# Keys and values projected on 64-row tiles, side by side on the two halves of TensorE's rows

## The chip, the cores and the metric

The kernel runs on one core of one Trainium2 chip. The metric is the device time of the program in microseconds (us), as the median of several runs. A profiled execution has a span (from the first to the last instruction) and its own time, which is a little longer than its span.

## The reference

A gated cross-attention block and a mixture of experts, in float32. There are 32 batches of 56 query tokens and 1500 context tokens, 256 channels, 16 heads of 16.

```
x = x + tanh(g_xattn) * layernorm(rs * (softmax(q k^T / 4, masked) v  @ Wo.T + bo)) * gamma + beta
      with q = layernorm(x) @ Wq.T + bq,  k = ctx @ Wk.T + bk,  v = ctx @ Wv.T + bv
x = x + tanh(g_ffn) * sum over 2 of 8 experts of w_e * (relu(layernorm(x) @ w_fc[e])**2 @ w_proj[e])
```

Scores are scaled by 1/4 and clipped to -50..50, and the two experts of a token come from a softmax over its two largest router logits.

## The kernel before

**Tiling.** The batches are worked on in 16 pairs (`NP`). A batch's 1500 context tokens are three groups of 500 (`TG`), a group is four chunks of 125 (`TC`). So a pair has 6 groups (`PG`) and 24 chunks (`PC`), and its loop runs over `UN` = 12 steps u = 0 to 11. A step works on two chunks, and on half of the projections of the group that comes next. Context arrives already transposed (channels on the partitions), in 500 KB transfers into `raw`.

**Precision.** Float32 products are made of three fp32r products: each operand is split into a rounded part (hi) and a remainder (lo), and hi x hi, hi x lo and lo x hi are summed in PSUM. This goes for keys, values, scores and experts.

**A step on TensorE** (`pair`): scores of two chunks (`scores`: 24 matmuls, each with 64 rows of keys as weights and 224 columns of masked queries moving; the two halves of the rows write two different banks), then `k_proj` (six matmuls: 128 rows, 128 output rows, 500 columns), then `v_proj` (twelve matmuls: 128 rows, 125 tokens as weights, 256 columns moving), then in some steps one of five side operations, then `pv` of the two chunks of the step before (probabilities times values; 17 output rows each, four in a quadrant each, with a column of ones that gives the softmax sums). Side operations use PSUM tile `side_ps`, which is bank 0 of `k_ps`: `spread_sums` at u=1, `x_transpose` at u=3, `q_proj` at u=5, `out_proj` at u=7, `y_transpose` at u=11. In the first pair and in the last some of them are missing, so each runs 15 times.

**ScalarE**: the exponential of each chunk (`exps`), the rounded keys (`k_hi_evac`), the rounded context (`ctx_high`, once in two steps), and evacuations of side operations. **VectorE**: the clip of the probabilities (`clip`), the remainders of context and keys (`ctx_low`, `k_lo_evac`), values plus bias from PSUM (`v_evac_step`, into `vst`), and in `before_clips` the small work of layer norm, query splitting and normalisation, by step. **GpSimd**: three inverse square roots in a pair, the remainder of the expert weights, x plus beta. Every engine works its queue in the order in which the code is written; semaphores tie them together. TensorE's program is unrolled, those of ScalarE, VectorE and SyncE loop over pairs.

**Waits that matter here.** `v_proj` may start when `v_evac` says that VectorE has emptied the one bank of `v_ps`; `k_proj` when `k_lo` says so of its bank; the next use of bank 0 after a side operation waits for that one's evacuation (the table `freed`). `spread_sums` waits for `sum_split`, which VectorE gives after `o_evac_step` and `sums_split` of the last PV. `delta` on VectorE waits for `out_proj`.

After the attention loop, seven groups of 256 tokens go through 8 experts each; the change doesn't touch that phase.

Of the kernel before, what the change touches and what calls it, by code (L numbers as in the profile page):

```python
# [16 lines left out]
P = 128  # L17
KD = D // P
# [35 lines left out]
def gated_cross_attention_moe(nc, a, x1_dram, out):  # L54
# [5 lines left out]
    with ExitStack() as ctx:  # L60
# [136 lines left out]
        ctx_split = sem("ctx_split")  # L197
        kproj_done = sem("kproj_done")
        vproj_done = sem("vproj_done")
        k_hi = sem("k_hi")  # L200
        k_lo = sem("k_lo")
        v_evac = sem("v_evac")
# [163 lines left out]
        def _(pe):  # L366
# [19 lines left out]
            def v_proj(n, half, s):  # L386
# [8 lines left out]
                                   wv_hi[:, k, :], wv_lo[:, k, :], k == 0, k == KD - 1)  # L395
                last.then_inc(vproj_done, 1)

            def scores(i, c):

                n = i * PC + c  # L400
                b, g = c // NC, c // GC
                if c % NC == 0:
                    pe.wait_ge(q_ready, 4 * i + 2 * b + 2)
                if c % GC == 0:
                    pe.wait_ge(k_lo, KD * (i * PG + g + 1))
                wait(pe, exp_done, n - 1)
                cs = slice(c % GC * TC, (c % GC + 1) * TC)
                for m in range(KD):
                    for term, (k, q) in enumerate(((kh, q_hi), (kh, q_lo), (kl, q_hi))):
                        for r in range(2):  # L410
# [64 lines left out]
            def pair(i, first=False, final=False):  # L475
                freed = {}
                if not first:
                    freed.update({0: (ylo_done, i), 2: (sum_evac, i), 8: (dlt_evac, i)})
                if not final:
                    freed.update({4: (xT_done, i + 2), 6: (qT_done, i + 2)})  # L480
                for u in range(UN):
                    q, half = divmod(u, 2)
                    n = i * PG + q + 1
                    more = not (final and q == PG - 1)
                    scores(i, 2 * u)
                    if first and u == 0:
                        pe.wait_ge(v_evac, 2)
                    scores(i, 2 * u + 1)
                    if more:
                        k_proj(n, half, (q + 1) % 2, freed.get(u))  # L490
                        v_proj(n, half, (q + 1) % 2)
                        if half == 1:
                            pe.wait_ge(k_lo, KD * n + 1)
                    if u == 1 and not first:
                        spread_sums(i - 1)
                    if u == 3 and not final:
                        x_transpose(i + 1)
                    if u == 5 and not final:
                        q_proj(i + 1)
                    if u == 7 and not first:  # L500
                        out_proj(i - 1)
                    if u == 10 and final:
                        pe.wait_ge(ylo_done, NP - 1)
                        pe.wait_ge(wr_split, 18)
                        pe.wait_ge(k_lo, KD * B * NG)
                        for t in range(RT):
                            router(0, t)
                    if u == 11 and not first:
                        y_transpose(i - 1)
                    if first and u == 1:  # L510
                        pe.wait_ge(o_clear, 1)
                    if not (first and u == 0):
                        for d in (2, 1):
                            pv(*((i, 2 * u - d) if u > 0 else (i - 1, PC - d)))
# [76 lines left out]
        def _(act):  # L591
# [7 lines left out]
            def ctx_high(n, s, count):  # L599

                act.wait_ge(raw_in[s], 16 * count)
                wait(act, vproj_done, 2 * (n - 1))
                act.activation(c_hi[:, s, :, :], raw[:, s, :, :], ACT.Copy).then_inc(ctx_hi, 1)

# [52 lines left out]
            def pair(i, first=False, final=False):  # L657
                for u in range(UN):
                    q, half = divmod(u, 2)
                    if u == 0 and not final:  # L660
                        load_xq(i + 1)
                    if u == 10:
                        if not first:
                            store_x1(i - 1)
                        load_xr(i)
                        if not final:
                            load_matrix(i + 1)
                    if half == 0 and not (final and q >= PG - 2):
                        ctx_high(i * PG + q + 2, q % 2, i * NG + q // 2 + 2)
                    exps(i, 2 * u)  # L670
                    exps(i, 2 * u + 1)
                    if not (final and q == PG - 1):
                        k_hi_evac(i * PG + q + 1, half, (q + 1) % 2)
                    if u == 1:
                        if not first:
                            sums_spread(i - 1)
                        expert_hi(i)
                    if u == 3 and not final:
                        x_transposed(i + 1)
                    if u == 11 and not first:  # L680
                        y_transposed(i - 1)
                    if u == 11 and final:
                        second_of_two(0)

# [52 lines left out]
        def _(dve):  # L737
# [179 lines left out]
            def pair(i, first=False, final=False):  # L917
                for u in range(UN):
                    q, half = divmod(u, 2)
                    before_clips(i, u, first, final)  # L920
                    if not (final and q >= PG - 2):
                        ctx_low(i * PG + q + 2, half, q % 2)
                    clip(i, 2 * u)
                    clip(i, 2 * u + 1)
                    if not (final and q == PG - 1):
                        k_lo_evac(i * PG + q + 1, half, (q + 1) % 2)
                        v_evac_step(i * PG + q + 1, half, (q + 1) % 2)
                if not first:
                    y_low(i - 1)

            def before_clips(i, u, first, final):

# [21 lines left out]
                    inverse(i - 1, 3)  # L954
                if u == 5 and not first:
                    divide(i - 1)
                if u == 6 and not final:
                    q_evac(i + 1)
                    q_split(i + 1, 0)
                if u == 7:  # L960
                    o_evac_step(i, 0)
                    sums_split(i, 0)
                    if not final:
                        q_high(i + 1, 0)
                if u == 8:
                    if not first:
                        delta(i - 1)
# [168 lines left out]
```

## Time and profile before

| | |
|---|---|
| time, 3 runs | median 1268.37 us (1267.36 to 1270.18) |
| profiled execution | 1267.26 us, span 1265.1 us |
| TensorE matmuls (PE) | 1248.7 us busy, 99% of the span |
| TensorE weight loads (PEld) | 1129.9 us, 89% |
| VectorE (DVE) | 964.8 us, 76% |
| ScalarE (ACT) | 688.5 us, 54% |
| GpSimd (POOL) | 174.6 us, 14% |
| HBM read and written | 60.77 MB and 3.67 MB, 51 GB/s over the span |
| mean granted TensorE clock | 0.997 of full speed |

The attention loop takes some 1070 us of the span, the experts the last 180. Busy time of PE is modelled, since matmuls overlap: the starts of matmuls and weight loads tell more than their durations. A weight load (LDWEIGHTS) brings the stationary operand into the array, and the matmul behind it streams the moving one.

### The profile page before, as it was taken

What the parts mean: (1) busy time and instruction counts of PE and PEld (TensorE: products, weight loads), DVE (VectorE), ACT (ScalarE), POOL (GpSimd) and SP (SyncE); (2) the same over time, 40 slices, a digit from 0 to 9 for tenths busy, and PEclk for the clock granted to TensorE, in tenths of its full rate; (3) what the DMA queues carried; (4) which work ended last, traced back from release to release, by engine and by line L of the source; (5) the groups of instructions that cost most, each with busy time, mean ns of one, the idle gap of its engine ahead of it and who ended that gap; (6) DMA issues with size and microseconds to landing.
All of it is one profiled execution on the core that took longest, in us unless ns stands there. A gap on an engine that the chain in (4) does not pass through costs nothing.

```text
span 1265.1 us, 51469 instructions
## 1 busy us (share of the span) xinstructions
PE 1248.7 (99%) x22040; PEld 1129.9 (89%) x22040; DVE 964.8 (76%) x1806; ACT 688.5 (54%) x854; POOL 174.6 (14%) x142
## 2 busy tenths in 40 slices
PE   7999999999999999999999999999999999899998
PEld 6888888888888888888888888888888888899998
DVE  6678777878787877787777878787878777687555
ACT  5555555556555556565555555565555565344443
POOL 1000101010101010010001010101010100154443
PEclk9999999999999999999999999999999999899999
DMA  5121212121112112121211121211121120010000
GB/s 158 52 67 43 64 53 70 53 66 56 55 51 68 55 42 71 47 70 53 70 50 57 53 70 53 67 55 54 51 69 55 45 74 5 19 64 10 17 8 17
DMA packets 29507, 68.19 MB, mean 54 GB/s; under 512 B 6037, under 2 KB 13458, under 8 KB 29330
## 3 DMA queue, kind: packets, MB, share of 16 engines
q1 hardware_dynamic: 20450, 54.61, 14.2%
q10 hardware_dynamic: 8880, 10.75, 2.6%
q8 instruction: 168, 2.75, 0.9%
q14 instruction: 9, 0.07, 0.0%
HBM read 60.77 MB, written 3.67 MB: 51 GB/s over the span
## 4 chain that ended last, share of the span: by engine, by line
PE 94%; issue 2%; DVE 1%; POOL 1%; ACT 0%; DMA 0%; DVEq 0%; POOLq 0%; ACTq 0%
PE sc_ps L412 23%; PE o_ps L427 14%; PE k_ps L369 10%; PE v_ps L370 7%; PE v_ps L369 7%; PE v_ps L371 7%; PE k_ps L371 7%; PE k_ps L370 7%; PE sc_ps L369 3%; PE sc_ps L370 3%; PE sc_ps L371 3%; PE k_ps L444 1%; POOL h_lo L352 1%; PE k_ps L457 1%; DVE h_sq L1043 0%
## 5 line engine op out<-in xcount | busy, mean ns | idle before, releaser
L610 ACT ACTIVATE prob<-sc_ps,m_bias 125x896 f32<-125x896 f32 x384 | 366.3, 1005 | 321.8 <-PE sc_ps L412 321.8
L915 DVE TENSOR_SCALAR prob<-prob 125x896 f32<-125x896 f32 x384 | 245.1, 642 | 140.8 <-ACT prob L610 137.4
L412 PE MATMUL sc_ps<-q_hi,kh 64*125 64x224 f32 x1536 | 228.5, 294 | 0.0
L370 PE MATMUL v_ps<-wv_lo,c_hi 128*125 128x256 f32 x764 | 214.8, 281 | 0.0
L369 PE MATMUL v_ps<-wv_hi,c_hi 128*125 128x256 f32 x764 | 214.3, 280 | 0.0
L371 PE MATMUL v_ps<-wv_hi,c_lo 128*125 128x256 f32 x764 | 214.0, 280 | 0.0
L412 PE MATMUL sc_ps<-q_hi,kl 64*125 64x224 f32 x1536 | 209.8, 270 | 0.0
L412 PE MATMUL sc_ps<-q_lo,kh 64*125 64x224 f32 x1536 | 209.3, 269 | 0.0
L427 PE MATMUL o_ps<-prob,vst 125*17 125x56 f32 x12288 | 189.2, 214 | 0.0
L427 PEld LDWEIGHTS o_ps<-prob,vst 125*17 125x17 f32 x12288 | 158.3, 98 | 31.5 <-issue 9.8
L763 DVE SCALAR_TENSOR_TENSOR kl<-k_ps,cst,kh 128x500 fp32r<-128x500 f32 x192 | 141.5, 738 | 46.5 <-ACT kh L597 44.7
L369 PE MATMUL k_ps<-c_hi,wk_hi 128*128 128x500 f32 x384 | 169.7, 442 | 0.9 <-DVE c_lo L769 0.9
L412 PEld LDWEIGHTS sc_ps<-q_hi,kh 64*125 64x125 f32 x1536 | 144.8, 185 | 17.7 <-issue 0.2
L597 ACT ACTIVATE kh<-k_ps,cst 128x500 fp32r<-128x500 f32 x192 | 130.5, 680 | 43.3 <-PE k_ps L371 41.0
L371 PE MATMUL k_ps<-c_hi,wk_lo 128*128 128x500 f32 x384 | 149.6, 390 | 0.0
L370 PE MATMUL k_ps<-c_lo,wk_hi 128*128 128x500 f32 x384 | 149.3, 389 | 0.0
L370 PEld LDWEIGHTS v_ps<-wv_lo,c_hi 128*125 128x125 f32 x764 | 141.8, 186 | 7.6
L369 PEld LDWEIGHTS v_ps<-wv_hi,c_hi 128*125 128x125 f32 x764 | 141.9, 186 | 7.2
L316 POOL TENSOR_TENSOR rstd<-var_e,mhalf 112x1 f32<-112x1 f32 x48 | 69.2, 1442 | 560.1 <-DVE var_e L753 560.1
L412 PEld LDWEIGHTS sc_ps<-q_hi,kl 64*125 64x125 f32 x1536 | 145.9, 187 | 0.0
L412 PEld LDWEIGHTS sc_ps<-q_lo,kh 64*125 64x125 f32 x1536 | 145.4, 186 | 0.0
L371 PEld LDWEIGHTS v_ps<-wv_hi,c_lo 128*125 128x125 f32 x764 | 141.9, 186 | 0.0
(129 smaller groups left out, 1913.7 us busy)
## 6 DMA issues: line engine op xcount, KB each, us to landing
raw<-in_ctxT SPq DMA_DIRECT2D x96, 500.0 KB, 3.5
w_raw<-in_we ACTq DMA_DIRECT2D x16, 256.0 KB, 3.7
xq<-in_x ACTq DMA_DIRECT2D x16, 112.0 KB, 2.0
xr<-in_x ACTq DMA_DIRECT2D x16, 112.0 KB, 3.6
x_scratch<-x ACTq DMA_DIRECT2D x16, 112.0 KB, 3.7
out_y<-acc SPq DMA_DIRECT2D x7, 256.0 KB, 2.0
acc<-x_scratch SPq DMA_DIRECT2D x1, 1280.0 KB, 6.3
rec<-rec SPq DMA_DIRECT2D x64, 14.0 KB, 2.3
```

What stands on the lines that cost most here:

```text
L316: pool.tensor_tensor(rstd[ln][0:PW, :], var_e[ln][0:PW, :], mhalf[0:PW, :], ALU.pow)\
L352: pool.tensor_tensor(h_lo[:, e % NB, :, :], h_sq[:, e % 2, :, :], plain(h_hi[:, e % NB, :, :]), ALU.subtract).then_inc(hlo_done, 1)
L369: pe.matmul(ps, w_h, m_h, start=first, stop=False)
L370: pe.matmul(ps, w_h, m_l, start=False, stop=False)
L371: return pe.matmul(ps, w_l, m_h, start=False, stop=last)
L412: last = pe.matmul(sc_ps[0:TC, 2 * (c % 2) + r, m * HS * S:(m + 1) * HS * S], k[rows, g % 2, m, cs], q[rows, b, m, :, :], start=term == 0, ...
L427: last = pe.matmul(o_ps[q * 32:q * 32 + VW, col * S:(col + 1) * S], vst[0:TC, c // GC % 2, c % GC, h, :], prob[0:TC, c % PB, at * S:(at + ...
L444: last = pe.matmul(bank[:, m * PW:(m + 1) * PW], wq[:, k, m * P:(m + 1) * P], xnT[:, k, :], start=(k == 0), stop=(k == KD - 1))
L597: act.activation(kh[:, s, m, :], k_ps[:, m, 0:TG], ACT.Identity, bias=bk[:, m:m + 1]).then_inc(k_hi, 1)
L610: act.activation(prob[0:TC, c % PB, :].rearrange("p (c n) -> p c n", c=2), sc_ps[0:TC, 2 * (c % 2):2 * (c % 2) + 2, 0:NH * S // 2], ACT.Ex ...
L763: dve.scalar_tensor_tensor(kl[:, s, m, :], k_ps[:, m, 0:TG], bk[:, m:m + 1], plain(kh[:, s, m, :]), ALU.add, ALU.subtract).then_inc(k_lo, 1)
L915: dve.tensor_scalar(p, p, EXP_LO, EXP_HI, ALU.max, ALU.min).then_inc(clip_done, 1)
```

## The change

Keys and values of a half group are computed by `kv_part`, in two parts. In part 0 the key matmuls use rows 0 to 63 (the first 64 of each 128 input channels) and the value matmuls rows 64 to 127; in part 1 it is the other way round, and each bank ends with the whole sum. Within a part the order is value (first chunk), key, value (second chunk), six times over. Part 0 stands at the head of a step, ahead of the first chunk's scores, part 1 between the two chunks' scores. The side operations now follow part 0. New semaphores `kpart_done` and `vpart_done` keep part 1 from starting before part 0 is complete, as both write the same banks. ScalarE and VectorE are reordered to suit: evacuations of keys and values stand between the two exponentials (clips), values ahead of the keys' remainder; evacuations of side operations, `q_evac` and `delta` come earlier.

```diff
+            def kv_part(n, half, s, part, side=None):
+                if part == 0:
+                    if half == 0:
+                        pe.wait_ge(ctx_split, KD * (n + 1))
+                    if side:
+                        wait(pe, *side)
+                    wait(pe, k_lo, KD * (n - 1) + half + 1)
+                    wait(pe, v_evac, 2 * n + half)
+                else:
+                    pe.wait_ge(kpart_done, 2 * (n - 1) + half + 1)
+                    pe.wait_ge(vpart_done, 2 * (n - 1) + half + 1)
+                k_rows = slice(part * HW, (part + 1) * HW)
+                v_rows = slice((1 - part) * HW, (2 - part) * HW)
+                ws = slice(half * P, (half + 1) * P)
+                for k in range(KD):
+                    k_terms, v_terms = kv_terms(s, k)
+                    for t in range(3):
+                        begin, end = part == 0 and k == 0 and t == 0, part == 1 and k == KD - 1 and t == 2
+                        w, c_m = k_terms[t]
+                        c_s, w_m = v_terms[t]
+                        for j in range(2):
+                            cs = slice((2 * half + j) * TC, (2 * half + j + 1) * TC)
+                            v_last = pe.matmul(v_ps[0:TC, j * D:(j + 1) * D], c_s[v_rows, cs], w_m[v_rows, k, :],
+                                               start=begin and j == 0, stop=end, skip_group_check=True)
+                            if j == 0:
+                                k_last = pe.matmul(k_ps[:, half, 0:TG], w[k_rows, k, ws], c_m[k_rows, :],
+                                                   start=begin, stop=end)
...
# TensorE, pair()
-                    scores(i, 2 * u)
-                    if first and u == 0:
-                        pe.wait_ge(v_evac, 2)
-                    scores(i, 2 * u + 1)
                     if more:
-                        k_proj(n, half, (q + 1) % 2, freed.get(u))
-                        v_proj(n, half, (q + 1) % 2)
+                        kv_part(n, half, (q + 1) % 2, 0, freed.get(u))
                         if half == 1:
                             pe.wait_ge(k_lo, KD * n + 1)
...
+                    if u == 11 and not first:
+                        y_transpose(i - 1)
+                    scores(i, 2 * u)
+                    if more:
+                        kv_part(n, half, (q + 1) % 2, 1)
+                    if first and u == 0:
+                        pe.wait_ge(v_evac, 2)
+                    scores(i, 2 * u + 1)
...
# ScalarE, ctx_high() and pair()
+                wait(act, kproj_done, KD * (n - 1))
...
                     exps(i, 2 * u)
-                    exps(i, 2 * u + 1)
-                    if not (final and q == PG - 1):
-                        k_hi_evac(i * PG + q + 1, half, (q + 1) % 2)
...
+                    if not (final and q == PG - 1):
+                        k_hi_evac(i * PG + q + 1, half, (q + 1) % 2)
+                    exps(i, 2 * u + 1)
...
# VectorE, pair() and before_clips()
                     clip(i, 2 * u)
+                    if u == 11 and not first:
+                        y_low(i - 1)
+                    if not (final and q == PG - 1):
+                        v_evac_step(i * PG + q + 1, half, (q + 1) % 2)
+                        k_lo_evac(i * PG + q + 1, half, (q + 1) % 2)
                     clip(i, 2 * u + 1)
...
+                if u == 5 and not final:
+                    q_evac(i + 1)
...
+                if u == 7 and not first:
+                    delta(i - 1)
                 if u == 7:
                     o_evac_step(i, 0)
                     sums_split(i, 0)
```

On TensorE, before, at u=1 of a pair: the last keys, the values (12 rows, two of them here), the spread of the sums, PV, and the next step's scores.

```order
L370 MATMUL k_ps<-c_lo,wk_hi 128x500
L371 MATMUL k_ps<-c_hi,wk_lo 128x500
L369 MATMUL v_ps<-wv_hi,c_hi 125x256
L370 MATMUL v_ps<-wv_lo,c_hi 125x256
...
L451 MATMUL k_ps<-sum_hi,sumsel_r 128x448
L452 MATMUL k_ps<-sum_lo,sumsel_r 128x448
L427 MATMUL o_ps<-prob,vst 17x56 x32
L412 MATMUL sc_ps<-q_hi,kh 125x224 x2
L412 MATMUL sc_ps<-q_lo,kh 125x224 x2
```

The same place in the changed program: the end of part 0 (L428 is the value matmul, L431 the key matmul), the spread of the sums, the scores of the first chunk, part 1.

```order
L428 MATMUL v_ps<-wv_lo,c_hi 125x256
L428 MATMUL v_ps<-wv_hi,c_lo 125x256
L431 MATMUL k_ps<-c_hi,wk_lo 128x500
L428 MATMUL v_ps<-wv_hi,c_lo 125x256
L493 MATMUL k_ps<-sum_hi,sumsel_r 128x448
L494 MATMUL k_ps<-sum_lo,sumsel_r 128x448
L454 MATMUL sc_ps<-q_hi,kh 125x224 x2
L454 MATMUL sc_ps<-q_lo,kh 125x224 x2
L454 MATMUL sc_ps<-q_hi,kl 125x224 x2
```

The spread now stands between two pieces of 64-row work, where it stood between 128-row values and PV; PV comes after part 1 and the second chunk's scores.

On VectorE, before, around u=7 and u=8 of a pair: clips of two chunks, the keys' remainder, the values, then `delta` (dlt from k_ps).

```order
L814 TENSOR_TENSOR q_hi<-q_rnd,cst 128x448
L769 TENSOR_TENSOR c_lo<-raw,c_hi 128x500
...
L915 TENSOR_SCALAR prob<-prob 125x896
...
L763 SCALAR_TENSOR_TENSOR kl<-k_ps,cst,kh 128x500
...
L778 TENSOR_TENSOR vst<-v_ps,rowv 125x32x16
L846 SCALAR_TENSOR_TENSOR dlt<-k_ps,rs,rowv 112x256
L748 BN_STATS st_1<-dlt 112x6
```

The same engine in the changed program, at u=7.

```order
L959 TENSOR_SCALAR prob<-prob 125x896
L890 SCALAR_TENSOR_TENSOR dlt<-k_ps,rs,rowv 112x256
...
L866 COPY ctxo<-o_ps 128x4x56
L873 CAST sum_hi<-ctxo 128x4x56
...
L875 TENSOR_TENSOR sum_lo<-ctxo,sum_hi 128x4x56
...
L858 TENSOR_TENSOR q_hi<-q_rnd,cst 128x448
L813 TENSOR_TENSOR c_lo<-raw,c_hi 128x500
...
L959 TENSOR_SCALAR prob<-prob 125x896
...
L822 TENSOR_TENSOR vst<-v_ps,rowv 125x32x16
```

`delta` stands ahead of u=7's other work instead of behind its values, and one clip, not two, stands ahead of the values.

## Rows read from the trace of the kernel before

**Rows 1.** The page, part 4: shares of the chain that ended last.

```profile
PE 94%; issue 2%; DVE 1%; POOL 1%; ACT 0%; DMA 0%; DVEq 0%; POOLq 0%; ACTq 0%
```

**Rows 2.** Windows of one pair: busy time of each engine, granted clock, DMA.

```profile
400.00:467.00 67.00, 67.00 (x1291) 59.69 (x1290) 53.24 (x100) 38.66 (x46) 6.56 (x5) 1.00 0.19 58
```

**Rows 3.** TensorE's waits, whole span: us in total, times, longest.

```profile
PE k_ps L451 <- DVE sum_lo L831: 2.7, 1, 2.7
```

**Rows 4.** Timeline of one step: start us, us, engine, line, operation.

```profile
402.16 0.37 PE L412 MATMUL sc_ps<-q_hi,kh 64*125 64x224 f32 x2
402.36 0.27 PE L412 MATMUL sc_ps<-q_lo,kh 64*125 64x224 f32 x2
402.37 0.19 PEld L412 LDWEIGHTS sc_ps<-q_hi,kl 64*125 64x125 f32 x2
402.47 0.27 PE L412 MATMUL sc_ps<-q_hi,kl 64*125 64x224 f32 x2
...
403.46 0.27 PE L412 MATMUL sc_ps<-q_hi,kl 64*125 64x224 f32 x2
403.66 0.19 PEld L369 LDWEIGHTS k_ps<-c_hi,wk_hi 128*128 128x128 f32 x1
403.77 0.19 PEld L370 LDWEIGHTS k_ps<-c_lo,wk_hi 128*128 128x128 f32 x1
...
405.12 0.28 PE L369 MATMUL v_ps<-wv_hi,c_hi 128*125 128x256 f32 x1
...
406.42 0.28 PE L371 MATMUL v_ps<-wv_hi,c_lo 128*125 128x256 f32 x1
406.63 0.98 PE L427 MATMUL o_ps<-prob,vst 125*17 125x56 f32 x64
406.82 0.69 DVE L778 TENSOR_TENSOR vst<-v_ps,rowv 125x512 f32<-125x512 f32 x1
407.54 0.37 PE L412 MATMUL sc_ps<-q_hi,kh 64*125 64x224 f32 x2
```

**Rows 5.** Timeline around two side operations, u=1 and u=7.

```profile
428.15 0.28 PE L371 MATMUL v_ps<-wv_hi,c_lo 128*125 128x256 f32 x1
428.27 0.36 PE L451 MATMUL k_ps<-sum_hi,sumsel_r 128*128 128x448 f32 x1
428.77 0.98 PE L427 MATMUL o_ps<-prob,vst 125*17 125x56 f32 x64
...
462.08 1.02 PE L457 MATMUL k_ps<-wo,rec 128*112 128x256 f32 x4
463.04 0.98 PE L427 MATMUL o_ps<-prob,vst 125*17 125x56 f32 x64
```

**Rows 6.** The page, part 5: busy us, mean ns, idle before.

```profile
L610 ACT ACTIVATE prob<-sc_ps,m_bias 125x896 f32<-125x896 f32 x384 | 366.3, 1005 | 321.8 <-PE sc_ps L412 321.8
L915 DVE TENSOR_SCALAR prob<-prob 125x896 f32<-125x896 f32 x384 | 245.1, 642 | 140.8 <-ACT prob L610 137.4
```

**Rows 7.** Timeline of VectorE at u=1, u=2 and u=8.

```profile
424.03 0.39 DVE L822 COPY ctxo<-o_ps 128x224 f32<-128x224 f32 x1
...
424.77 0.39 DVE L831 TENSOR_TENSOR sum_lo<-ctxo,sum_hi 128x224 fp32r<-128x224 f32 x1
...
425.08 0.62 DVE L814 TENSOR_TENSOR q_hi<-q_rnd,cst 128x448 fp32r<-128x448 f32 x1
425.61 0.67 DVE L769 TENSOR_TENSOR c_lo<-raw,c_hi 128x500 fp32r<-128x500 f32 x1
...
429.17 0.42 DVE L748 BATCH_NORM_STATS2 st<-xq 112x6 f32<-112x256 f32 x1
...
431.20 1.00 DVE L769 TENSOR_TENSOR c_lo<-raw,c_hi 128x500 fp32r<-128x500 f32 x1
432.13 1.70 DVE L915 TENSOR_SCALAR prob<-prob 125x896 f32<-125x896 f32 x2
...
463.15 0.48 DVE L846 SCALAR_TENSOR_TENSOR dlt<-k_ps,rs,rowv 112x256 f32<-112x256 f32 x1
```

More of the change, by code:

```diff
@@ L199, in gated_cross_attention_moe @@
         vproj_done = sem("vproj_done")
+        kpart_done = sem("kpart_done")
+        vpart_done = sem("vpart_done")
         k_hi = sem("k_hi")
@@ L396, in v_proj, with kv_terms @@
                 last.then_inc(vproj_done, 1)
+            def kv_terms(s, k):
+                return ((wk_hi, c_hi[:, s, k, :]), (wk_hi, c_lo[:, s, k, :]), (wk_lo, c_hi[:, s, k, :])), \
+                       ((c_hi[:, s, k, :], wv_hi), (c_hi[:, s, k, :], wv_lo), (c_lo[:, s, k, :], wv_hi))
+            def kv_part(n, half, s, part, side=None):
[25 more added lines that the diff above has]
+                                                   start=begin, stop=end)
+                if part == 0:
+                    k_last.then_inc(kpart_done, 1)
+                    v_last.then_inc(vpart_done, 1)
+                else:
+                    k_last.then_inc(kproj_done, 1)
+                    v_last.then_inc(vproj_done, 1)
             def scores(i, c):
@@ L507, in pair @@
                             router(0, t)
-                    if u == 11 and not first:
-                        y_transpose(i - 1)
                     if first and u == 1:
@@ L670, in pair @@
                     exps(i, 2 * u)
-                    exps(i, 2 * u + 1)
-                    if not (final and q == PG - 1):
-                        k_hi_evac(i * PG + q + 1, half, (q + 1) % 2)
[L674 to L677, printed above, removed]
+                    if u == 1 and not first:
+                        sums_spread(i - 1)
                     if u == 3 and not final:
@@ L681, in pair @@
                         y_transposed(i - 1)
+                    if not (final and q == PG - 1):
+                        k_hi_evac(i * PG + q + 1, half, (q + 1) % 2)
+                    exps(i, 2 * u + 1)
+                    if u == 1:
+                        expert_hi(i)
                     if u == 11 and final:
@@ L923, in pair @@
                     clip(i, 2 * u)
-                    clip(i, 2 * u + 1)
[L925 to L929, printed above, removed]
+                    if u == 11 and not first:
[3 more added lines that the diff above has]
+                        k_lo_evac(i * PG + q + 1, half, (q + 1) % 2)
+                    clip(i, 2 * u + 1)
             def before_clips(i, u, first, final):
@@ L956, in before_clips @@
                     divide(i - 1)
+                if u == 5 and not final:
+                    q_evac(i + 1)
                 if u == 6 and not final:
-                    q_evac(i + 1)
                     q_split(i + 1, 0)
+                if u == 7 and not first:
+                    delta(i - 1)
                 if u == 7:
@@ L966, in before_clips @@
                     if not first:
-                        delta(i - 1)
                         delta_statistics(i - 1)
```

## The prediction

> **What bounds the kernel now.** I read the chain of waits first: 94% of it is TensorE [rows 1]. Then the stretch 400 to 467 us, one pair of batches: TensorE is busy 67.00 of 67.00 us, VectorE 53.24, ScalarE 38.66, at the full granted clock [rows 2]. Then TensorE's waits: the one of 2.7 us lies in the expert phase at the end, and the list has none from the attention loop [rows 3]. So this kernel is bound by TensorE's own stream, and the question is what one step (half a group) of that stream is made of. The timeline gives it, 402.16 to 407.54, 5.38 us [rows 4]. The reader is to look at starts, not durations (ends are modelled):
> - scores: a pair of 64-row matmuls every 0.110 us (402.36 to 403.46, ten steps). The next pair's weights start loading at 402.37, right behind the matmuls of 402.36, and are used at 402.47: a load needs 0.10 us, so this stream is paced by its loads.
> - scores to keys: from the last pair (403.46) to the first key load (403.66) 0.20, and the second load only comes at 403.77. Against an unbroken 0.11 that is 0.09 of draining and 0.11 of uncovered load: **a switch costs 0.20**.
> - keys: six matmuls of 500 columns from 403.77 to 405.12, 0.225 each. Values: 405.12 to 406.42, eleven steps, 0.118 each.
> - values to probabilities-times-values (PV): 0.21 instead of 0.118, then PV takes 0.91 (406.63 to 407.54) and the next step's first score load is exposed as the first key load is. Three switches in each step.
>
> **Part by part.** *Streams.* Each key matmul (128 rows) becomes two of 64 rows, each value matmul too, so TensorE issues twice as many. A group of three in the new code is value, key, value, the two values on one half of the rows, the key on the other. The trace shows 64-row matmuls on the two halves running beside each other (a pair in 0.110 us though 224 columns are streamed twice), but never with unequal lengths. If the value row runs as it does now, a group takes 2 x 0.118 = 0.236, and the key (0.225) is covered. Twelve groups: 2.84. Now: 6 x 0.225 + 12 x 0.118 = 2.77. **+0.07 a step**, times 190 steps (192 less the last two, which project nothing) = +13 us. The bound below: a value matmul can't come faster than its load lets it, 0.109 as in the scores, which gives 0.218 a group; the bound above, with the two rows in each other's way, 0.250 (between 0.236 and the 0.343 of full serialisation, nearer the first, because the scores show so little interference). I take 0.236, since the 256-column row is measured at this width, and nothing in the score rows shows 64 rows going faster per column.
> The page "TensorE: Matmul & The Clock Gate" of the Trainium skill (Part 3, what overlaps and what doesn't) says a weight load overlaps a running matmul only where the row group differs. That would put both value loads of a group in the open, 2 x (0.118 + 0.10) = 0.44 a group, and the sum some 460 us higher. The trace disagrees for the present streams: the score load of 402.37 starts 0.01 behind matmuls on the very same rows [rows 4].
>
> *The switch that goes.* Key and value parts now have the scores' 64-row shape, so scores to keys costs no switch: 0.09 + 0.106 (a score load, 403.66 to 403.77 here) = 0.196, x 190 = **-37 us**.
>
> *The switches that come.* Five side operations in each pair (spread sums, x transpose, q projection, output projection, y transpose) are 128-row or 112-row work. Today they follow the values at an unbroken 0.12 (428.15 to 428.27) and end in the switch to PV that was due anyway [rows 5]. In the change they stand between part 0 and the scores, both 64-row. Each pays a switch in and one out that no other work covers: +2 x 0.19 (0.08 or 0.09 draining, 0.10 load), 75 times (five in fifteen pairs): **+28.5 us**. So 190 switches go and 150 come, and the two terms together are -8.5, not -37.
>
> *Waits that come.* The release to VectorE comes 0.40 after a last start (values 406.42, vst 406.82). Now vst has all of PV, scores and keys, 3.9 us, before TensorE's next value matmul needs the bank. In the change the next value matmul is the first thing behind the scores and PV. Plain step of the change, from its first load: part 0 starts at 0.10, scores 1.52, part 1 2.18, scores 3.60, PV 4.35, next step 5.26. Exponential of chunk 2u: ready 2.48, ends 3.49; its clip 4.13; vst 4.83 (1.005 and 0.64 [rows 6], 0.69 [rows 4]). Slack 0.4, and VectorE comes free at 0.95 of the next step (last score start 4.15, + 0.40 + 1.005 + 0.64 = 6.2). So steps in which VectorE has more than some 2 us ahead of the clip stall TensorE, and everything behind it:
> - u=1: spread sums needs sum_lo. VectorE starts ctxo at 0.95, and sum_lo ends 1.13 later (424.03 to 424.77 + 0.39 [rows 7]), 2.1. TensorE is there at 1.60. Wait 0.5. Before, it came 4.5 us after PV.
> - u=2: VectorE, free at 1.1, has 2.03 from st to c_lo (429.17 to 431.20), then c_lo at 1.00 instead of 0.67, as GpSimd is at work beside it, a clip of 0.85 (two in 1.70), vst 0.69: 5.7 against 5.26. Wait 0.45.
> - u=7: delta is now ahead of o_evac in VectorE's queue and waits for the output projection, which starts at 1.70; dlt follows a start by 1.07 (462.08 to 463.15 [rows 5, 7]): 2.77, +0.48, +1.67 (424.03 to 425.08 + 0.62), + c_lo 0.67, + clip 0.64, + vst 0.69 = 6.9 against 6.5 (5.26 + 0.96 + 0.28). Wait 0.4.
> - u=3: x transpose waits for xn, 0.1. (u=9 and u=11 come out within 0.1 of their slack.)
> Together 1.5 x 15 = **+23 us**. Bounds: 0 if VectorE is quicker in all four, 35 if u=9 and u=11 join with 0.4 each.
>
> *At nothing:* kpart_done and vpart_done (0.66 of scores cover a release of 0.40); without that cover 0.2 x 190 = 38 us. ctx_high's wait for keys as well as values (both end together; ScalarE is idle 40% of the time). Moving k_lo_evac behind v_evac (0.7 later, still over 1 us ahead of the next scores that need it). No DMA is moved past a wait that matters. The prologue and the expert phase keep their instructions.
>
> *Sum* against the profiled execution's own 1267.3: -37 + 28.5 + 13 + 23 = +27.5, 1294.8. The median of the runs is 1.1 above the profiled one: **1296**.
>
> **Rivals.**
> *Faster streams (other side).* If 64-row value matmuls run at 0.109, a group is 0.218: 190 x 12 x 0.018 = -41. A step of 5.04 leaves VectorE 0.2 less, which puts some 10 back. -31: 1265; and 1240 if of the waits only the one for sum_lo stays. It decides from 0.224 a group down. For it: the score pairs do keep 0.110 with no sign of a limit but the load. Against: 500 columns at 0.225 and 256 at 0.118 lie on one line of 0.44 ns a column, which a load can't explain. The Trainium skill's page "TensorE: Matmul & The Clock Gate" (Part 2, back-to-back issue gap) gives N / 2.4 + 2.5 ns, 109 for 256 columns; the row of values has 118 [rows 4]; by that rule the sum would be 1255 before any waits are added back. Chance 0.15.
> *Serialised.* The second value matmul of a group waits for the key matmul ahead of it in the queue, 0.225 + 0.118 = 0.343 a group: +243, 1538. For it: no row shows tiles of unequal length in flight. Against: in the scores two matmuls share one start of 0.110 each, so the halves don't wait for each other. Chance 0.10.
> *Waits hidden.* VectorE is idle 14 us a pair; if the four waits vanish, 23 less: 1273. Chance 0.15.
> *Rows in each other's way*, 0.250 a group: +32, 1327. Chance 0.08.
> *Forecast as worked out,* 1280 to 1315: 0.52.
>
> **How the numbers follow.** A measurement of this kernel tells about 0.2% (2.5 us) from no change. Slower: the forecast, serialised, rows in each other's way, nearly all of waits hidden: 0.76. Faster: most of faster streams, 0.16. Within: 0.08. The range leaves out the serialised case and the low tail of the fast one (0.18 together): 1260 to 1327.
>
> **What the profile will show.** Right: starts of value matmuls at 0.118 in pairs with one key start in 0.236; no gap of 0.20 between scores and parts; a gap of 0.20 and an exposed load on both sides of each side operation; a plain step of 5.26 instead of 5.38; TensorE waits for vst, at steps 3 and 8 above all, and for sum_lo, about 0.5 each. Wrong: a group at 0.22 or at 0.34; side operations that follow part 0 at 0.12; no TensorE waits on VectorE at all.

## The result: 1286.3 us, 1.4% slower

| | before | changed |
|---|---|---|
| median of 4 runs each | 1267.86 us | 1286.27 us (1285.23 to 1286.6) |
| profiled execution, span | 1267.26, 1265.1 us | 1286.42, 1284.2 us |

The ratio is 1.014 with a 95% interval of 1.0123 to 1.0158. The forecast was 1296, in the range 1260 to 1327.

The page of the changed kernel, parts 1 and 4 (compare [rows 1]): TensorE's part of the chain has fallen by 5 points, and those of VectorE (1 to 4%) and ScalarE (0 to 2%) have grown.

```profile
PE 1249.5 (97%) x25460; PEld 1178.5 (92%) x25460; DVE 928.3 (72%) x1806; ACT 700.6 (55%) x854; POOL 163.5 (13%) x142
...
PE 89%; DVE 4%; issue 3%; ACT 2%; POOL 1%; DMA 0%; ACTq 0%; DVEq 0%; POOLq 0%
```

TensorE's waits in the changed kernel (us in total, times, longest). There are three kinds in the attention loop now: the sums (10.8, of which 2.7 were there before), the values' bank, and in the first step of all the context's remainder, which part 0 at the head of a step wants before the first scores. Of these the kernel before had only the last, and shorter; [rows 3] doesn't show it:

```profile
PE k_ps L369 <- DVE c_lo L769: 0.9, 1, 0.9
```

The changed kernel:

```profile
PE k_ps L493 <- DVE sum_lo L875: 10.8, 16, 2.7
...
PE v_ps L428 <- DVE vst L822: 6.9, 15, 0.5
PE v_ps L428 <- DVE c_lo L813: 2.6, 1, 2.6
```

The stretch of 67 us, as [rows 2]: TensorE is no longer busy all of it.

```profile
400.00:467.00 67.00, 65.86 (x1495) 61.53 (x1492) 50.12 (x98) 39.10 (x46) 5.79 (x5) 1.00 0.20 58
```

A plain step of the changed kernel on TensorE's timeline, PV to PV, answering to [rows 4] (L428 values, L431 keys, L454 scores, L469 PV):

```profile
414.98 0.98 PE L469 MATMUL o_ps<-prob,vst 125*17 125x56 f32 x64
415.89 0.38 PE L428 MATMUL v_ps<-wv_hi,c_hi 64*125 64x256 f32 x1
...
416.46 0.38 PE L431 MATMUL k_ps<-c_hi,wk_lo 64*128 64x500 f32 x1
416.47 0.39 PE L428 MATMUL v_ps<-wv_hi,c_lo 64*125 64x256 f32 x2
416.68 0.39 PE L431 MATMUL k_ps<-c_hi,wk_hi 64*128 64x500 f32 x1
416.70 0.39 PE L428 MATMUL v_ps<-wv_hi,c_hi 64*125 64x256 f32 x2
...
417.14 0.39 PE L431 MATMUL k_ps<-c_hi,wk_lo 64*128 64x500 f32 x1
417.17 0.40 PE L428 MATMUL v_ps<-wv_hi,c_lo 64*125 64x256 f32 x2
417.37 0.30 PE L454 MATMUL sc_ps<-q_hi,kh 64*125 64x224 f32 x2
...
417.91 0.31 PE L454 MATMUL sc_ps<-q_hi,kl 64*125 64x224 f32 x2
418.02 0.28 PE L428 MATMUL v_ps<-wv_hi,c_hi 64*125 64x256 f32 x1
...
419.97 0.27 PE L454 MATMUL sc_ps<-q_hi,kl 64*125 64x224 f32 x2
420.17 0.93 PE L469 MATMUL o_ps<-prob,vst 125*17 125x56 f32 x60
```

The reader is to see three things. Pairs of value matmuls start 0.235 apart (416.47, 416.70, and 417.17 two groups on), and keys beside them 0.22 to 0.23 apart: the two halves of the rows run side by side with unequal lengths. The first score starts 0.08 behind the last value (417.29, the second of the pair at 417.17): it runs on the half that had the keys, 0.23 behind the last of them (417.14), which is their own pace. Part 1 follows the scores after 0.11. So there is no switch at either seam. The step takes 5.19 us, against 5.38 before and 5.26 in the forecast.

One more thing stands in these rows. A pair of scores is one matmul on each half. Between the parts a pair lasts 0.30 to 0.31 from its first start to its second end, at the end of the step 0.27: its two matmuls start 0.04 apart at 417.37 (417.373 and 417.413) and still so at 417.91, and 0.01 apart at 419.97. So the half that had the keys, which were done sooner, keeps its lead through the scores, and loses it in part 1, where it has the values.

Now step 1 of a pair, where the sums are spread, and the head of step 3:

```profile
433.34 0.40 PE L428 MATMUL v_ps<-wv_hi,c_lo 64*125 64x256 f32 x2
433.74 0.39 DVE L875 TENSOR_TENSOR sum_lo<-ctxo,sum_hi 128x224 fp32r<-128x224 f32 x1
434.27 0.44 PE L493 MATMUL k_ps<-sum_hi,sumsel_r 128*128 128x448 f32 x1 [0.54 <-DVE sum_lo L875]
...
439.69 1.29 POOL L328 TENSOR_TENSOR we_lo<-w_raw,we_hi 128x512 f32 x1 [24.31 <-ACT we_hi L681]
...
440.30 1.17 DVE L858 TENSOR_TENSOR q_lo<-q_rem,cst 128x448 fp32r<-128x448 f32 x1
440.94 0.93 POOL L318 TENSOR_TENSOR rstd<-var_e,mhalf 112x1 f32<-112x1 f32 x1
...
442.15 0.97 DVE L813 TENSOR_TENSOR c_lo<-raw,c_hi 128x500 fp32r<-128x500 f32 x1
442.94 0.98 PE L469 MATMUL o_ps<-prob,vst 125*17 125x56 f32 x64
443.04 0.61 DVE L959 TENSOR_SCALAR prob<-prob 125x896 f32<-125x896 f32 x1
443.57 0.68 DVE L822 TENSOR_TENSOR vst<-v_ps,rowv 125x512 f32<-125x512 f32 x1
444.40 0.35 PE L428 MATMUL v_ps<-wv_hi,c_hi 64*125 64x256 f32 x1 [0.47 <-DVE vst L822]
```

Both are as foreseen in place and kind. TensorE stands at the sums for 0.54. At step 2 VectorE's q_lo and c_lo take 1.17 and 0.97 beside GpSimd (we_lo, then rstd and, from 441.84, x plus beta), where they take 0.62 and 0.67 alone, so the clip and vst are late. The forecast had counted the slower c_lo and not the slower q_lo, which in the kernel before met GpSimd only in its last 0.3 us and took 0.62. PV starts at 442.94, the values behind it at 444.40: 1.46 instead of the 0.91 of a plain step (414.98 to 415.89).

**Where 19 us came from**, from the starts of PV in one pair (u: 12 steps, us; medians over the pairs). Before: seven plain steps at 5.38, and with a side operation 5.79, 5.60, 6.26, 6.26 and 5.60 (u=1, 3, 5, 7, 11), 67.2 together. Changed: six plain at 5.19 to 5.21, with side operations 6.60 (u=1), 6.31 (u=3), 6.50 (u=5), 6.49 (u=7), 5.79 (u=11), and 5.38 at u=8, 68.2 together.

| term, us a pair | worked out | forecast | measured |
|---|---|---|---|
| switch and streams, 12 steps | 5.19 - 5.38 | -1.5 | -2.3 |
| side operations, switches in and out | 5 x 0.38 forecast; 0.47, 0.36, 0.43, 0.42 and 0.38 measured (u=1, 3, 5, 7, 11) | +1.9 | +2.1 |
| waits | u=1 0.54, u=3 0.54, u=8 0.20 | +1.5 | +1.3 |
| sum | | +1.9 | +1.1 |

A side operation's price is here what its step has over a plain step, less its wait, less the same excess in the kernel before.

The whole of it, between the profiled executions (19.2), by the starts of PV again: the 14 pairs between the first and the last add 14.9. The first pair, which has two side operations and not five, gives 0.3 back, and the last adds 0.6. The other 4.0 are there before the first PV (30.8 us, against 26.8). Of these 1.7 is the longer wait for c_lo (2.6 against 0.9). Some 1.0 has nothing to do with the change: the prologue's 128-row keys and values, the same in both programs, end that much later, since in this execution the keys start 0.42 apart until 14.0 us, and before until 12.0. And behind the wait the clock fell: TensorE had stood idle for 2.55, and from 21 to 24 us its granted clock is 0.50 (1.2 GHz), where the kernel before has 1.00 in the same stretch. Pairs of values start 0.43 apart there, not 0.235, which costs some 1.7 (an estimate: half of the time from 20.9 to 24.3 us, for which that pace lasts). These three make 4.4, so 0.4 come back somewhere in the first step; that isn't split up.

```profile
21.00:24.00 3.00, 3.00 (x29) 3.00 (x27) 1.54 (x7) 0.01 (x1) 0.00 (x0) 0.50 0.61 176
```

### The profile page after: what moved, and what is told of

It is laid out like the page before. It is cut to its first block, busy times and chain, and to the rows that moved or that the text cites. A ratio compares the mean times of both kernels' runs of the same rounds, so it can differ in the third digit from the quotient of the medians.

```text
span 1284.2 us, 58772 instructions
## 1 busy us (share of the span) xinstructions
PE 1249.5 (97%) x25460; PEld 1178.5 (92%) x25460; DVE 928.3 (72%) x1806; ACT 700.6 (55%) x854; POOL 163.5 (13%) x142
## 4 chain that ended last, share of the span: by engine, by line
PE 89%; DVE 4%; issue 3%; ACT 2%; POOL 1%; DMA 0%; ACTq 0%; DVEq 0%; POOLq 0%
PE v_ps L428 23%; PE sc_ps L454 21%; PE k_ps L431 20%; PE o_ps L469 12%; PE sc_ps L371 3%; PE sc_ps L372 3%; PE sc_ps L373 3%; ACT prob L654 1%; PE k_ps L486 1%; PE k_ps L499 1%; POOL h_lo L354 1%; DVE vst L822 1%; PE k_ps L493 1%; DVE sum_lo L875 1%; DVE ctxo L866 0%
## 5 line engine op out<-in xcount | busy, mean ns | idle before, releaser
L428 PE MATMUL v_ps<-wv_hi,c_hi 64*125 64x256 f32 x1520 | 320.0, 290 | 11.3 <-DVE vst L822 6.9
L431 PE MATMUL k_ps<-c_hi,wk_hi 64*128 64x500 f32 x760 | 315.5, 415 | 0.0
L428 PE MATMUL v_ps<-wv_lo,c_hi 64*125 64x256 f32 x1520 | 301.6, 278 | 0.0
L428 PE MATMUL v_ps<-wv_hi,c_lo 64*125 64x256 f32 x1520 | 300.0, 277 | 0.0
L431 PE MATMUL k_ps<-c_lo,wk_hi 64*128 64x500 f32 x760 | 293.3, 386 | 0.0
L431 PE MATMUL k_ps<-c_hi,wk_lo 64*128 64x500 f32 x760 | 292.6, 385 | 0.0
L428 PEld LDWEIGHTS v_ps<-wv_hi,c_hi 64*125 64x125 f32 x1520 | 225.3, 183 | 29.9 <-issue 12.7
L454 PE MATMUL sc_ps<-q_hi,kh 64*125 64x224 f32 x1536 | 234.7, 277 | 0.1
L428 PEld LDWEIGHTS v_ps<-wv_hi,c_lo 64*125 64x125 f32 x1520 | 229.3, 183 | 0.0
L454 PE MATMUL sc_ps<-q_lo,kh 64*125 64x224 f32 x1536 | 229.1, 270 | 0.0
L428 PEld LDWEIGHTS v_ps<-wv_lo,c_hi 64*125 64x125 f32 x1520 | 228.9, 183 | 0.0
L454 PE MATMUL sc_ps<-q_hi,kl 64*125 64x224 f32 x1536 | 228.8, 269 | 0.0
L454 PEld LDWEIGHTS sc_ps<-q_hi,kh 64*125 64x125 f32 x1536 | 196.4, 185 | 16.0 <-issue 10.0
L469 PE MATMUL o_ps<-prob,vst 125*17 125x56 f32 x12288 | 189.1, 214 | 0.0
L469 PEld LDWEIGHTS o_ps<-prob,vst 125*17 125x17 f32 x12288 | 158.2, 98 | 21.8
L454 PEld LDWEIGHTS sc_ps<-q_hi,kl 64*125 64x125 f32 x1536 | 165.2, 186 | 0.0
L454 PEld LDWEIGHTS sc_ps<-q_lo,kh 64*125 64x125 f32 x1536 | 164.2, 185 | 0.0
L431 PEld LDWEIGHTS k_ps<-c_lo,wk_hi 64*128 64x128 f32 x760 | 141.5, 186 | 0.0
```

The lines of the kernel that those rows point to most:

```text
L428: v_last = pe.matmul(v_ps[0:TC, j * D:(j + 1) * D], c_s[v_rows, cs], w_m[v_rows, k, :], start=begin and j == 0, stop=end, skip_group_check ...
L431: k_last = pe.matmul(k_ps[:, half, 0:TG], w[k_rows, k, ws], c_m[k_rows, :], start=begin, stop=end)
L469: last = pe.matmul(o_ps[q * 32:q * 32 + VW, col * S:(col + 1) * S], vst[0:TC, c // GC % 2, c % GC, h, :], prob[0:TC, c % PB, at * S:(at + ...
```

## Experiments

Every run was timed beside the kernel before on the same chip, and ratios are to that. The theory: a row-shape switch costs 0.20 and each side operation between 64-row pieces costs two of them; groups run at the values' own 0.236; the rest is waits for VectorE.

**1. Side operations into the middle of the scores, in the kernel before.** Four of the five move; the spread of the sums stays.

```diff
 # before, TensorE, pair()
                     scores(i, 2 * u)
+                    if half == 1 and more:
+                        pe.wait_ge(k_lo, KD * n + 1)
+                    if u == 3 and not final:
+                        x_transpose(i + 1)
...
+                    if u == 11 and not first:
+                        y_transpose(i - 1)
...
                     scores(i, 2 * u + 1)
```

> The kernel before, with four of its five side operations (x transpose, q projection, output projection, y transpose) moved from behind the values to between the scores of the two chunks, that is, between 64-row work on both sides; nothing else moves. Theory: each such place costs two switches of TensorE's row shape that had no cost where it stood, 0.38 us, 60 times, so +23 us on the kernel before, 1291. Rival: the 0.20 us seen between scores and keys belongs to the first key load alone (a 128-column load of full rows behind a wait), and short side operations slip in at their own length: within 5 us of the kernel before.

1290.7 us, ratio 1.0166 (1.0149 to 1.0183) on 1269.9: +20.8 of 23 expected. Its timeline at u=3 (PV, scores, the transpose, scores):

```profile
442.81 0.98 PE L427 MATMUL o_ps<-prob,vst 125*17 125x56 f32 x64
...
444.36 0.27 PE L412 MATMUL sc_ps<-q_hi,kl 64*125 64x224 f32 x2
444.56 0.41 PE L436 MATMUL k_ps<-cst,xn 112*128 112x112 f32 x2
444.90 0.37 PE L412 MATMUL sc_ps<-q_hi,kh 64*125 64x224 f32 x2
445.11 0.27 PE L412 MATMUL sc_ps<-q_lo,kh 64*125 64x224 f32 x2
```

Scores to transpose takes 0.20 (444.36 to 444.56), not 0.11, and behind the transpose the first pair of scores takes 0.21, not 0.11, since its load is in the open. The step is 5.92, against 5.60 with the transpose in its old place: 0.32; the projections cost 0.39 and 0.36 by the same reading. In the kernel before, where TensorE's tiling of keys and values is untouched, this shows the switch to be the price of the place.

**2. The spread of the sums behind the first chunk's scores.**

```diff
-                    if u == 1 and not first:
-                        spread_sums(i - 1)
...
                     scores(i, 2 * u)
+                    if u == 1 and not first:
+                        spread_sums(i - 1)
                     if more:
                         kv_part(n, half, (q + 1) % 2, 1)
```

> The changed kernel, with the spread of the sums at step 1 moved behind the first chunk's scores (before part 1). Theory: TensorE there no longer waits for the last sum_lo (10.8 us of waits in the changed kernel's list, 2.7 of them in the expert phase), so 8 to 9 us less than the changed kernel, 1277 to 1278, with the same number of switches. Rival: VectorE is what paces these steps, and the wait comes back at the next values: no change, 1286.

1278.3 us, ratio 1.0067 (1.0051 to 1.0084): as expected, 8 less than the changed kernel. Step u=1 takes 6.03 instead of 6.60. In the list the wait for the sums is down to the one of 2.7 us that was there before, and that for vst stays at 6.9.

**3. One key matmul in six.** This leaves out five sixths of the key projection.

```diff
-                            if j == 0:
+                            if j == 0 and k == 0 and t == 0:
                                 k_last = pe.matmul(k_ps[:, half, 0:TG], w[k_rows, k, ws], c_m[k_rows, :],
-                                                   start=begin, stop=end)
+                                                   start=begin, stop=part == 1)
```

> The changed kernel with one key matmul in six left in each part (the other five are left out, so keys are only a fraction of their sum). Theory: a group of value, key, value takes 0.236 us because the value row streams 2 x 256 columns at its own pace, and the key row beside it costs nothing: same as the changed kernel, 1283 to 1287. Rival: the two rows share something (reading, writing), so values alone would fall to what a load allows, 0.218 a group: 41 us less, 1245.

1264.4 us, ratio 0.996 (0.9946 to 0.9974): neither. Its timeline at the end of part 0:

```profile
402.48 0.39 PE L428 MATMUL v_ps<-wv_hi,c_lo 64*125 64x256 f32 x2
402.71 0.39 PE L428 MATMUL v_ps<-wv_hi,c_hi 64*125 64x256 f32 x2
402.94 0.28 PE L428 MATMUL v_ps<-wv_lo,c_hi 64*125 64x256 f32 x1
402.95 0.36 PE L454 MATMUL sc_ps<-q_hi,kh 64*125 64x224 f32 x1
403.06 0.28 PE L428 MATMUL v_ps<-wv_lo,c_hi 64*125 64x256 f32 x1
403.16 0.28 PE L454 MATMUL sc_ps<-q_lo,kh 64*125 64x224 f32 x1
403.18 0.28 PE L428 MATMUL v_ps<-wv_hi,c_lo 64*125 64x256 f32 x1
```

The pairs of values still start 0.23 to 0.24 apart with nothing beside them, so the pace is theirs, and the rival (0.218) falls. But the idle half of the rows doesn't wait: the first score on it starts at 402.95, ahead of three value matmuls that stand before it in the program (403.06, 403.18, 403.30). The halves run ahead of each other across instructions, and a plain step takes 4.96 to 5.00 us. The lead is short: each half has lost five keys a step, 1.1 us, and the step gains only 0.2. Steps with a side operation gain nothing (6.62, 6.52, 6.50, 6.49 and 5.79), and TensorE's wait for vst rises from 6.9 to 10.4.

This is what the forecast had missed, and the rows of the unaltered plain step above show it too. Values and keys change halves between the parts, and the scores between don't bring the halves into step. So what a half loses to 0.236 of values in one part it gets back with 0.227 of keys in the other: a step costs a half six keys and twelve values, 1.36 + 1.42 = 2.78, not 2.84. The 0.06 agrees with the measured step, 5.19 and not 5.26.

**4. The new order with full rows.** Keys and values in one piece of 128 rows at the head of a step.

```diff
-                        kv_part(n, half, (q + 1) % 2, 0, freed.get(u))
+                        k_proj(n, half, (q + 1) % 2, freed.get(u))
+                        v_proj(n, half, (q + 1) % 2)
...
                     scores(i, 2 * u)
-                    if more:
-                        kv_part(n, half, (q + 1) % 2, 1)
```

> The changed kernel's order on all engines, but with keys and values as full 128-row matmuls in one piece at the head of a step, where part 0 stands. Theory: the order by itself costs nothing, since side operations then follow 128-row work again and TensorE reaches the spread of the sums and the next values late enough: as the kernel before, 1268 (within 3). Rival: the new order of exponentials, clips and evacuations costs time whatever the tiling: 1278 or more.

1302.4 us, ratio 1.0261 (1.0243 to 1.0278): the theory falls. Plain steps are back at 5.38 and side operations cost no extra switch, but a pair takes 69.1 us, 1.9 more than before. The longest of the waits, at the head of u=0, behind the y transpose of u=11:

```profile
430.40 1.01 ACT L653 ACTIVATE prob<-sc_ps,m_bias 125x896 f32<-125x896 f32 x1 [3.11 <-PE sc_ps L454]
430.86 0.98 PE L469 MATMUL o_ps<-prob,vst 125*17 125x56 f32 x64
431.31 0.35 ACT L671 ACTIVATE yT_hi<-k_ps 128x224 f32 x1
...
431.98 0.38 DVE L912 TENSOR_TENSOR yT_lo<-k_ps,yT_hi 128x224 f32 x1
...
432.47 0.46 PE L371 MATMUL k_ps<-c_hi,wk_hi 128*128 128x500 f32 x1 [0.63 <-issue]
```

yT_hi stands behind an exponential, which waits for scores that now come after the transpose. yT_lo waits for yT_hi, and the next keys need the bank. By starts of keys and side operations the heads of u=0, 8, 2 and 3 lose 0.70, 0.40, 0.25 and 0.1, and the sums 0.46. So the order by itself costs 33 us, and the 64-row tiling in two parts takes 16 of them back. It puts a chunk of scores and half of the projections between a side operation and the next use of its bank. How much of the 16 comes from that distance and how much from the switches isn't shown: no run has two parts with full rows.

**5. VectorE's work moved, TensorE's order kept.**

```diff
 # VectorE, before_clips()
 # u == 1, behind q_high(i, 1); taken from u == 2
+                    if not final:
+                        dve.wait_ge(xq_in, 16 * (i + 2))
+                        statistics(0, i + 1, xq)
...
-                if u == 7 and not first:
-                    delta(i - 1)
                 if u == 7:
                     o_evac_step(i, 0)
                     sums_split(i, 0)
...
+                if u == 7 and not first:
+                    delta(i - 1)
```

> The changed kernel with two edits on VectorE alone: the layer norm statistics of the next pair move from step 2 to step 1 (behind q_high), and delta moves behind o_evac, sums and q_high at step 7. TensorE's order stays. Theory: the two waits of TensorE for vst, 0.54 us ahead of step 3 and 0.20 ahead of step 8, go: 0.74 x 15 = 11 us less than the changed kernel, 1275. Rival: both waits only move on (to step 2's own values, or to step 8's output), less than 3 us gained.

1273.7 us, ratio 1.0055 (1.004 to 1.007): 12.5 less, 11 expected. Of the 15 waits for vst in the list one of 0.4 is left, and the steps u=3 and u=8 take 5.79 and 5.19. By starts of PV a pair takes 67.51 instead of 68.24, 11.0 us in 15 pairs. The rest lies ahead of anything that the edit touches: the first PV of this profiled execution comes at 28.3 us and not at 30.8, in the main because behind the same wait for c_lo (2.6) the granted clock stays at 1.00 from 21 to 24 us.

**6. The two projections ahead of PV.**

```diff
 # TensorE
-                    if u == 5 and not final:
-                        q_proj(i + 1)
-                    if u == 7 and not first:
-                        out_proj(i - 1)
...
                     scores(i, 2 * u + 1)
+                    if u == 5 and not final:
+                        q_proj(i + 1)
+                    if u == 7 and not first:
+                        out_proj(i - 1)
 # VectorE: q_evac(i + 1) at u == 5 and delta(i - 1) at u == 7 behind k_lo_evac, ahead of clip(i, 2 * u + 1)
```

> The changed kernel with the q projection and the output projection (steps 5 and 7) moved from behind part 0 to between the second chunk's scores and PV, and q_evac and delta on VectorE ahead of that step's last clip. Theory: there a side operation adds one switch, not two (the one out of it takes the place of the one into PV): 0.19 x 2 x 15 = 6 us less, and the wait of 0.20 ahead of step 8 goes too, 3 us: 1277. Rival: the next part 0 now waits for q_evac or delta, since bank 0 is wanted 1.1 us after the side operation: no gain, 1286 or more.

1275.2 us, ratio 1.0061 (1.0045 to 1.0076): 11 less, 9 expected, and 9.4 by starts of PV (67.61 a pair). The step with the q projection:

```profile
451.06 0.98 PE L469 MATMUL o_ps<-prob,vst 125*17 125x56 f32 x64
456.27 1.15 PE L486 MATMUL k_ps<-xnT,wq 128*128 128x112 f32 x8
457.34 0.98 PE L469 MATMUL o_ps<-prob,vst 125*17 125x56 f32 x64
```

From PV to PV 6.28, against 6.50 in the changed kernel (454.44 to 460.94, with the projection at 456.96): one switch less, 0.22. The step u=8 is back at 5.18.

**7. Spread late, statistics at step 1, projections ahead of PV, together.** The edits are those of 2, 5 (without its delta) and 6.

> The changed kernel with three edits together: spread of the sums behind the first chunk's scores, q and output projections ahead of PV, statistics of the next pair at step 1. Theory: the gains add, 8 for the spread, 8 for the statistics, 9 for the projections: 1261, under the kernel before (1269). Rival: VectorE is late somewhere else as steps get shorter: 1268 or more.

1260.5 us, ratio 0.9943 (0.9929 to 0.9956): 1261 expected, and faster than the kernel before. In its list of TensorE's waits one of 0.4 is left for vst, and of the sums only the one of 2.7 us that was there before. By starts of PV a pair takes 66.5 us, against 67.2 before the change.

**8. The y transpose ahead of PV too.**

```diff
 # TensorE: y_transpose(i - 1) at u == 11 from behind part 0 to behind scores(i, 2 * u + 1)
 # ScalarE: y_transposed(i - 1) from ahead of k_hi_evac to behind it
 # VectorE: y_low(i - 1) from ahead of v_evac_step to behind k_lo_evac
```

> As the three edits together, and the y transpose too moves ahead of PV, with its two evacuations behind the keys' and ahead of the last exponential and clip of step 11. Theory: one switch less, 0.19 x 15 = 3 us less than the three edits: 1258. Rival: the next pair's part 0 needs bank 0 before y_low is through (1.5 us after the last score, against 1.55 by the same count), and the later exponential makes VectorE late at step 0: same or slower than the three edits.

1260.6 us, ratio 0.9952 (0.9938 to 0.9965): the rival. The transpose's step gains 0.25 (5.54 instead of 5.79), and part 0 behind it starts late:

```profile
417.10 0.98 PE L469 MATMUL o_ps<-prob,vst 125*17 125x56 f32 x64
...
417.29 0.36 ACT L672 ACTIVATE yT_hi<-k_ps 128x224 f32 x1 [0.40 <-PE k_ps L505]
...
417.81 0.39 DVE L913 TENSOR_TENSOR yT_lo<-k_ps,yT_hi 128x224 f32 x1
...
418.31 0.35 PE L428 MATMUL v_ps<-wv_hi,c_hi 64*125 64x256 f32 x1 [0.23 <-issue]
```

1.21 from PV to values, not 0.91: 0.30 lost for 0.25 gained.

**9 and 10. Part 1 right behind part 0**, first with the evacuations left where they were, then with them moved.

```diff
 # 9 and 10, TensorE
-                    scores(i, 2 * u)
                     if more:
                         kv_part(n, half, (q + 1) % 2, 1)
+                    scores(i, 2 * u)
 # 10 alone, ScalarE: exps(i, 2 * u) behind k_hi_evac
 # 10 alone, VectorE: clip(i, 2 * u) behind v_evac_step and k_lo_evac
```

> The changed kernel with part 1 moved from between the two chunks' scores to right behind part 0 (behind the side operation where there is one), so that nothing stands between the two parts in 115 of the 190 steps. Theory: part 1 waits there for part 0's completion, which releases 0.40 us after a last start, and then loads weights in the open, 0.10: 0.50 instead of the unbroken 0.118, so +0.38 x 115 = +44 us on the changed kernel; values are complete one chunk of scores earlier, so the waits for vst (0.74 a pair, 11 us) go: 1319. Rival: as the two halves of the rows run independently, the pause is filled by the half that is ahead, and only the vst waits change: 1275 to 1286.

1530.2 us, ratio 1.2075 (1.2054 to 1.2097): far outside both. I had counted the pause between the parts and forgotten the queue. On VectorE vst stands behind the clip of chunk 2u, which waits for its exponential, which waits for scores that now come after part 1. The row of TensorE's waits:

```profile
PE v_ps L428 <- DVE vst L822: 191.6, 189, 1.8
```

> Part 1 right behind part 0 as in the run before, with the evacuations put where they can then be done: on ScalarE the keys (and side operations) ahead of the first exponential of the step, on VectorE values and keys' remainder ahead of the first clip. Theory: what cost 1.05 us a step there was that vst stood behind a clip that waited for scores which by then came after part 1; without that queueing only the pause between the parts is left (0.45 from the last start to the next first load's, +0.10 of load, against 0.118: 0.44 in 115 steps, +50) and the old waits for vst (11) are gone: 1325. Rival: VectorE and ScalarE simply can't turn values round in the 2.2 us of scores and PV: 1400 or more.

1332.4 us, ratio 1.051 (1.0493 to 1.0528): near the 1325 expected, and the vst waits are gone from the list. That for the sums has grown from 10.8 to 14.6. The pause itself (part 0's last values, part 1's first):

```profile
411.35 0.40 PE L428 MATMUL v_ps<-wv_hi,c_lo 64*125 64x256 f32 x2
411.89 0.35 PE L428 MATMUL v_ps<-wv_hi,c_hi 64*125 64x256 f32 x1
412.08 0.27 PE L428 MATMUL v_ps<-wv_hi,c_hi 64*125 64x256 f32 x1
```

The second matmul of the pair at 411.35 starts 0.12 later, at 411.47. The next start stands 0.42 behind that, and from it to the second value are 0.19 instead of 0.12, since its load was in the open: 0.37 lost in all. A plain step takes 5.63, 0.44 more than 5.19; that the remaining 0.07 is the half in arrears, which now has to be waited for, is argued and not shown. The scores between the parts are what hides this, 0.44 a step, where the forecast had put 0.2 on the loss of that cover.

## Why the prediction was right, and where it was off

**The two prices of the switch** held. Scores to keys costs none in the new tiling, and each side operation between 64-row pieces costs 0.36 to 0.47 against the 0.38 forecast; experiment 1 shows the same price without the new tiling (0.32 to 0.39), experiment 6 shows one switch to be worth 0.22. The page "TensorEngine Tiling (Array Packing)" of the Trainium skill (Key Properties) says that changing the tiling mode drains the engine. With that the traces agree, and they add a number: 0.20 to 0.21 where the row shape changes, against 0.11 where it doesn't (experiment 1).

**Streams.** The group of 0.236 held to the hundredth, and serialised and faster streams are both out. The term "+0.07 a step, +13 us" was mis-sized: it measured +0.01 a step, as the halves of the rows run on across the scores and change work between the parts (experiment 3). Between the profiled executions the forecast had +27.5 and 19.2 came. Streams and the switch that goes are 12 lower together, -36 and not -24. The side operations are 2.5 higher and the waits 4 lower, and some 5 from the prologue and the loop's ends stood nowhere in the forecast. So its total is closer than its terms: part of that is luck, as an error of 12 one way met some 4 the other way. The reading that the scores are paced by their loads isn't shown either. On the forecast's own line of 0.44 ns a column, 224 columns take 0.104 us, as long as the load. The Trainium skill's page "TensorE: Matmul & The Clock Gate" (Part 3, what overlaps and what doesn't) says that matmuls keep program order in start and end. The run with few keys disagrees across halves: a later score starts at 402.95, an earlier value at 403.06.

**Waits.** u=1 (0.5 forecast, 0.54), the head of u=3 (0.45 and 0.54), the head of u=8 (0.4 and 0.20) came where they were put; that for xn at u=3 did not show. Experiments 2 and 5 take them away one by one and gain what they were worth (8.0 and 11.0 us by the pairs). The forecast had +23 us and the pairs show 19. **The prologue** I had put at no change, since it keeps its instructions. But the first step of the loop wants c_lo earlier: +1.7 of wait, and behind it in this execution some 1.7 of half clock.

**"At nothing":** the two part semaphores are covered, as said, but the price without cover was too low by half (0.2 against 0.44 a step).

**What the forecast didn't ask** is how the order would do without the tiling. Experiment 4 says 33 us worse. So part of the two-part form's worth lies in bank and queue distances, not in TensorE's stream.

## What to carry to other kernels

Count switches of TensorE's row shape around a whole loop, not at the seam that a change removes: here 190 went and 150 came, because short 128-row operations were left in the middle of 64-row work. Put such operations at a seam where the shape changes anyway, and check that their bank isn't wanted before its evacuation, since one switch (0.2 us) is worth no more than a small wait. When work moves to the head of a step, write down for each evacuation what stands ahead of it in its own queue and what that in turn waits for: one clip ahead of vst turned a pause of 0.44 us into a step longer by 1.5.

## What the runs showed that I had not expected

The two halves of TensorE's rows run ahead of each other across instructions of different kinds: with one half idle, scores started on it while three earlier value matmuls were still to start on the other, and a plain step fell from 5.19 to 4.97 us.

What VectorE loses beside GpSimd depends on the operation. Its q_lo took 1.17 us beside we_lo (128x512) and rstd, and c_lo 0.97 beside x plus beta (112x256). Beside rstd alone, which has one value a row, q_lo kept its 0.62 in 14 cases and c_lo its 0.67 in 29.

A wait of 2.55 us on TensorE ahead of the first step was followed by a stretch at half the granted clock in one execution (the changed kernel's) and by none in another (experiment 5's). The four executions of experiment 5 differ in the same way: three of 1273.7 to 1273.8 us have a mean granted clock of 0.996, the one of 1275.8 has 0.994.
